# Two transformer layers in one kernel: the second batch stops preparing a third

## Chip, core and metric

The kernel runs on one core of one Trainium2 chip. The metric is the device time of one execution in microseconds (us), as the median of several runs. One more execution is taken with the hardware profiler; all rows below come from it.

## What is computed

Two layers on `x` of shape (2, 2048, 128), in float32. Each layer is an attention and a feed-forward part with adaptive layer norms (`mod` holds six rows for each batch) and residual adds. Cut to its steps:

```python
# layer 0
h = layernorm(x) * (1 + ca) + sa
Q, K, V = h @ Wq.T, h @ Wk.T, h @ Wv.T;  Q, K = rotate(Q), rotate(K)     # RoPE
x = x + ga * softmax(mask(Q @ K.T / sqrt(128), tril(k=1))) @ V
h = layernorm(x) * (1 + cb) + sb
x = x + gb * fp4_linear(silu(fp4_linear(h, w_gate)) * fp4_linear(h, w_up), w_down)
# layer 1
h = layernorm(x) * (1 + ca) + sa
x = x + ga * softmax(causal(h @ qk @ h.T / sqrt(128))) @ h @ ov
h = layernorm(x) * (1 + cb) + sb
x = x + gb * moe(h)      # 8 experts, top 2, each with one mean weight, plus a shared expert
```

## The kernel before

**Tiles and slots.** A batch has 2048 rows: 16 tiles of 128 rows, in 4 groups of 4. The queries of one tile are one slot. Slots 0 to 15 are the attention of layer 0, slots 16 to 31 that of layer 1, so a batch has 32 slots. The feed-forward part of layer 0 follows six and eight slots behind (`FFN_LAG`, `DOWN_LAG`), and norms and projections of later groups are spread over the slots by fixed slot numbers. All of it is written once for each engine in a loop `for b in range(BATCH)`, unrolled by Python, with BATCH = 2. After both batches the expert stage (moe) runs for all rows.

**In a slot.** PE computes the scores of the next slot in chunks of 512 keys (three passes for each chunk, `score_products`, L647), turns the probabilities of this slot (`turn_probs`, L755) and multiplies them with the values (`values`, L777). ACT computes the exponentials (`exp`, L1057) and copies what PE has turned out of the one PSUM bank TURN (`copy_probs`, L1083). DVE takes the maxima (`maximum`, L1357), adds the output to `x_sb` (`finish`, L1373) and does norms. POOL does the square roots for norms (`rsqrt`, L473).

**The order.** Each engine runs its own list in order. The scores of slot s+1 need the exponentials of slot s to have been read from the same banks (`exp_done`); transposes need bank TURN free again (`copied`). `TURN_AT` gives each turn of the bank its number in a batch (`turn_order`), and every wait on `turned` or `copied` counts `b * IN_TURN + TURN_AT[key]`. DVE's own order is counted by `dve_step`, 185 steps for each batch (`STEPS_PER_BATCH`).

**Preparing the next batch.** From slot 26 on, a batch starts layer 0 of the next one, `batch = BATCH - 1 - b`, so that the next batch finds its first group ready. NEXT_SLOT is 28. In order:

- slots 26 and 28: DVE `first_statistics` of groups 0 and 1 (L1220), POOL a square root for each
- slots 27 and 29: DVE `first_normalise` (L1227) of groups 0 and 1
- slot 28: PE turns the first group (key `"next"`, L595), ACT copies it to `hT` (L1029), PE `project_0(0, 0)` for the keys (L606), DVE `first_rotate` (L1237 to L1242)
- slot 29: PE `project_0(0, 1)` for the queries (L606), DVE `first_rotate`
- after slot 31: PE `first_values_and_scores` (L665, L647 to L659), then nine filler products `keep_clock(GATE, 9)` (L601), then the turning of layer 1's last norm group, key `("norm3", 3)`, and its router `logits` (L844). ACT copies the values (L998) and computes the first exponentials (`first_exp`, L1005); DVE takes the first maximum (L1291).

The second batch (b = 1) does all of this too, for batch 0 again; nothing reads the result.

After the last logits DVE adds the bias (L1437), ACT loads a table and computes the sigmoid (L1130), DVE picks the experts (L1507 to L1532), and meanwhile PE turns the expert weights (L888) and runs 17 fillers; then it turns the picks (L895), and the expert stage begins (L922).

Of the kernel before, what the change touches and what calls it, by code (L numbers as in the profile page):

```python
# [98 lines left out]

def input_turns(slot):  # L100

    firsts = (("fp4_in", FFN_LAG), ("norm2", DOWN_LAG + GROUP + 1), ("norm3", TILES + GROUP + 2))
    turns = [(kind, group_at(slot, first)) for kind, first in firsts if group_at(slot, first) is not None]
    if slot == NEXT_SLOT:
        turns.append(("next", 0))
    return turns if early_group(slot, K0_SLOT) is None else [("norm0", early_group(slot, K0_SLOT))] + turns
# [23 lines left out]

def turn_order():


    order = []
    for s in range(SLOTS):
        order += input_turns(s)
        for c in range(len(turn_chunks(*divmod(s, TILES)))):
            order.append(("probs", s, c))
            if c == 0 and ffn_tile(s, DOWN_LAG) is not None:
                order.append(("hq", s - DOWN_LAG))  # L140
    return order + [("norm3", GROUPS - 1)]


TURN_AT = {key: n + 1 for n, key in enumerate(turn_order())}
IN_TURN = len(TURN_AT)

# [9 lines left out]
parts_before, MAX_PARTS = before(lambda l, i: len(score_chunks(l, i)) if len(score_chunks(l, i)) > 1 else 0)  # L156
STEPS_PER_BATCH = 185


def build(nc, x, cos, sin, wq, wk, wv, w_gate, w_up, w_down, c0, wmod0, qk, ov, gate_w, lb_bias,  # L160
          e_gate, e_up, e_down, s_gate, s_up, s_down, c1, wmod1, out):
    ctx = ExitStack()
    with ctx:
# [276 lines left out]
        def _(pool):  # L440
# [43 lines left out]
            for b in range(BATCH):  # L484
# [12 lines left out]
                def hq_scaled(n):  # L497
                    pool.wait_ge(hq_grid, b * TILES + n + 1)
                    if n >= 2:
                        pool.wait_ge(turned, b * IN_TURN + TURN_AT["hq", n - 2] + 1)  # L500
                    pool.tensor_tensor(hq[:, n % 2, :], ha[:], hp[:], ALU.add).then_inc(hq_step, 1)  # L501
                    pool.wait_ge(hq_step, b * 2 * TILES + 2 * n + 1)
                    pool.tensor_tensor(hq[:, n % 2, :], hq[:, n % 2, :], hp[:], ALU.subtract).then_inc(hq_step, 1)
                    pool.wait_ge(hq_step, b * 2 * TILES + 2 * n + 2)
                    blocks = hq[:, n % 2, :].rearrange("p (k e) -> p k e", e=BLOCK)
                    pool.tensor_tensor(blocks, blocks, qh[:, 2, :].unsqueeze(2).to_broadcast(
                        [P, INNER // BLOCK, BLOCK]), ALU.mult).then_inc(hq_ready, 1)

                def xq_scaled(g):
                    pool.wait_ge(xq_grid, b * GROUPS + g + 1)  # L510
                    if g >= 1:
                        pool.wait_ge(turned, b * IN_TURN + TURN_AT["fp4_in", g - 1] + 1)
                    pool.tensor_tensor(xq[:], qa[:], qp[:], ALU.add).then_inc(xq_step, 1)
                    pool.wait_ge(xq_step, b * 2 * GROUPS + 2 * g + 1)
                    pool.tensor_tensor(xq[:], xq[:], qp[:], ALU.subtract).then_inc(xq_step, 1)
                    pool.wait_ge(xq_step, b * 2 * GROUPS + 2 * g + 2)
                    blocks = xq[:].rearrange("p (k e) -> p k e", e=BLOCK)
                    pool.tensor_tensor(blocks, blocks, qs[:, 2, :].unsqueeze(2).to_broadcast(
                        [P, GROUP * P // BLOCK, BLOCK]), ALU.mult).then_inc(xq_ready, 1)
# [13 lines left out]
                def keys_low(g):  # L533

                    cols = slice(g * BANK, (g + 1) * BANK)
                    pool.wait_ge(copied, b * IN_TURN + TURN_AT["norm2", g] + 1)
                    pool.tensor_tensor(h_parts[1][:, cols], hT[:, cols], h_parts[0][:, cols].bitcast(F32),
                                       ALU.subtract).then_inc(keys_ready, 1)

                for s in range(SLOTS):  # L540
# [13 lines left out]
                    if early_group(s, NORM0_SLOT) is not None:  # L554
                        rsqrt(2, early_group(s, NORM0_SLOT))
                    if s in (NEXT_SLOT - 2, NEXT_SLOT):
                        rsqrt(2, GROUPS + (s == NEXT_SLOT))
# [16 lines left out]
        def _(pe):  # L574
# [105 lines left out]
            for b in range(BATCH):  # L680
                def bank_free(key):

                    pe.wait_ge(copied, b * IN_TURN + TURN_AT[key])

                def out_of_bank(key):

                    pe.wait_ge(copied, b * IN_TURN + TURN_AT[key] + 1)

# [20 lines left out]
                def project_0_in(s):  # L709
# [13 lines left out]
                    if q is not None:  # L723
                        pe.wait_ge(roped, b * 4 * GROUPS + 4 * q + 2)
                        project_0(q, 1)
                    if s == NEXT_SLOT:
                        out_of_bank(("next", 0))
                        pe.wait_ge(logits_sum, b * GROUPS + GROUPS - 2)
                        project_0(0, 0)
                    if s == NEXT_SLOT + 1:  # L730
                        pe.wait_ge(roped, (b + 1) * 4 * GROUPS + 2)
                        project_0(0, 1)
# [102 lines left out]
                def logits(g):  # L835
                    out_of_bank(("norm3", g))
                    if g == 0:
                        pe.wait_ge(gu_used, b * TILES + TILES)
                    if g >= GROUPS - 2:
                        pe.wait_ge(roped, (b + 1) * 4 * GROUPS + 4)  # L840
# [8 lines left out]
                for s in range(SLOTS):  # L849
                    following = len(score_chunks(*divmod(s + 1, TILES))) if s + 1 < SLOTS else 0  # L850
                    n = len(turn_chunks(*divmod(s, TILES)))
                    for key in input_turns(s):
                        turn_group(key)
# [22 lines left out]
                pe.wait_ge(logits_sum, b * GROUPS + GROUPS - 1)  # L876
                first_values_and_scores(b, b * -1 + (BATCH - 1))
                keep_clock(GATE, 9)
                turn_group(("norm3", GROUPS - 1))
                pe.wait_ge(v_ready, (b + 1) * 2 * GROUPS + 1)  # L880
                logits(GROUPS - 1)


            pe.wait_ge(moe_w_loaded, 16 * 6)
            pe.wait_ge(logits_sum, BATCH * GROUPS)
            pe.wait_ge(copied, BATCH * IN_TURN + 1)
            for n in range(3 * UNITS):
# [70 lines left out]
        def _(act):  # L958
# [51 lines left out]
            for b in range(BATCH):  # L1010
                def filled(key):

                    act.wait_ge(turned, b * IN_TURN + TURN_AT[key] + 1)

# [34 lines left out]
                def exp(s, c):  # L1049
                    start, width = score_chunks(*divmod(s, TILES))[c]  # L1050
                    if c == 0:
                        act.wait_ge(max_ready, b * SLOTS + s + 1)
                        if s >= 2:
                            last = len(turn_chunks(*divmod(s - 2, TILES))) - 1
                            act.wait_ge(turned, b * IN_TURN + TURN_AT["probs", s - 2, last] + 1)
                    width = min(width, SEQ - start)
# [43 lines left out]
                for s in range(SLOTS):  # L1100
# [4 lines left out]
                    if n > 1:  # L1105
                        exp(s, 1)
                    for key in input_turns(s):
                        copy_group(key)
# [5 lines left out]
                    for c in range(max(n, turns)):  # L1114
# [6 lines left out]
                        if c + 2 < n:  # L1121
                            exp(s, c + 2)
                put_v_at(0, (b + 1) * 2 * GROUPS)
                copy_group(("norm3", GROUPS - 1))
                first_exp(b)
                act.wait_ge(copied, b * IN_TURN + IN_TURN + 1)

# [46 lines left out]
        def _(dve):  # L1174
# [3 lines left out]
            def link(ins):  # L1178

                steps[0] += 1  # L1180
                ins.then_inc(dve_step, 1)
                dve.wait_ge(dve_step, steps[0])
# [111 lines left out]
            first_maximum(-1)  # L1294
            setup_steps = steps[0]

            for b in range(BATCH):
                count = [0]

                def link(ins):  # L1300
                    count[0] += 1
                    ins.then_inc(dve_step, 1)
                    dve.wait_ge(dve_step, b * STEPS_PER_BATCH + setup_steps + count[0])

                def x_tile(t, n=1):
# [126 lines left out]
                def take_logits(g):  # L1432

                    dve.wait_ge(copied, b * IN_TURN + TURN_AT["norm3", g] + 1)
                    dve.tensor_copy(hT_all[:, bass.ds(b * SEQ + g * BANK, BANK)], hT_group[:])
# [16 lines left out]
                for s in range(SLOTS):  # L1452
# [9 lines left out]
                    if ffn_tile(s, FFN_LAG) is not None:  # L1462
                        combine(s - FFN_LAG)
                    if s in (NEXT_SLOT, NEXT_SLOT + 1):
                        first_rotate(b, s - NEXT_SLOT, link)
                    for c in range(1, following):
                        maximum(s + 1, c)
                    normalise_in_slot(s)
                    if s in (NEXT_SLOT - 1, NEXT_SLOT + 1):
                        first_normalise(b, BATCH - 1 - b, int(s > NEXT_SLOT))  # L1470
                    if ffn_tile(s, FFN_LAG) is not None:
                        quantise_h(s - FFN_LAG)
                    if early_group(s, NORM0_SLOT) is not None:
                        norm_0_statistics(early_group(s, NORM0_SLOT))
                    if s in (NEXT_SLOT - 2, NEXT_SLOT):
                        first_statistics(BATCH - 1 - b, int(s == NEXT_SLOT), link)
# [5 lines left out]
                normalise_in_slot(SLOTS + 1)  # L1482
                first_maximum(b)
                take_logits(GROUPS - 1)

                in_loop = count[0]
            assert in_loop == STEPS_PER_BATCH, in_loop

            steps[0] = setup_steps + BATCH * STEPS_PER_BATCH

            def link(ins):
                steps[0] += 1
                ins.then_inc(dve_step, 1)
                dve.wait_ge(dve_step, steps[0])


# [142 lines left out]
```

## Time and profile before

| | us |
|---|---|
| median of 3 runs | 732.59 |
| lowest, highest run | 732.2, 740.7 |
| profiled execution, whole | 740.21 |
| its span in the trace | 738.4 |

| engine | busy us | share of the span |
|---|---|---|
| PE | 647.3 | 88% |
| PE weight load | 504.9 | 68% |
| DVE | 511.4 | 69% |
| ACT | 319.5 | 43% |
| POOL | 222.5 | 30% |

The mean granted clock of PE is 0.948 of full speed. PE's products overlap one another, and their ends are modelled; the distance from one start to the next tells more than the length of one. The first batch runs to about 329 us, the second to about 620 us, the expert stage from about 634 us to the end.

### The profile page before, as it was taken

How to read it: one execution, taken by the hardware profiler on the slowest of the kernel's cores; microseconds unless marked ns; L12 is line 12 of the kernel's file. 1: busy time of each engine (PE TensorE's matmuls, PEld its weight loads, DVE VectorE, ACT ScalarE, POOL GpSimd, SP SyncE). 2: the span in 40 equal slices, each digit the busy share in tenths (PEclk: the TensorE clock that was granted, in tenths of full speed). 3: DMA queues.
4: the chain of work that ended last, by engine and by line, in shares of the span. 5: the costliest groups of instructions: out<-in, count | busy, mean ns of one | idle time of the engine just before them, and what ended most of it. 6: DMA issues, size and time to landing. Idle time of an engine off the chain costs nothing.

```text
span 738.4 us, 11039 instructions
## 1 busy us (share of the span) xinstructions
PE 647.3 (88%) x3816; PEld 504.9 (68%) x3828; DVE 511.4 (69%) x1465; ACT 319.5 (43%) x644; POOL 222.5 (30%) x225
## 2 busy tenths in 40 slices
PE   5889799988777999988889989958889998799997
PEld 4456687877556778775678777846677786576674
DVE  5957598696768667726669777596865754876665
ACT  1133344445234454543344444523445453554453
POOL 3333654343545211004455435253421102000000
PEclk9989999999879999999999999978999999999999
DMA  8400000000000000000000000000000000000001
GB/s 262 110 0 1 2 1 1 1 0 1 1 0 1 1 1 1 1 1 1 1 1 1 1 1 2 1 1 0 1 1 1 1 1 1 0 16 29 14 19 40
DMA packets 12078, 9.64 MB, mean 13 GB/s; under 512 B 1708, under 2 KB 10744, under 8 KB 12024
## 3 DMA queue, kind: packets, MB, share of 16 engines
q1 hardware_dynamic: 12024, 8.94, 4.1%
q8 instruction: 31, 0.51, 0.3%
q14 instruction: 23, 0.19, 0.1%
HBM read 6.84 MB, written 2.10 MB: 12 GB/s over the span
## 4 chain that ended last, share of the span: by engine, by line
PE 69%; DVE 18%; ACT 5%; POOL 4%; issue 4%; DMA 1%; SPq 0%; ACTq 0%; POOLq 0%
PE ps L777 14%; PE ps L647 12%; PE ps L755 8%; PE ps L606 5%; DVE xn L1320 5%; PE ps L922 4%; PE ps L924 4%; PE ps L923 4%; PE ps L800 3%; PE ps L665 2%; PE ps L801 2%; PE ps L595 2%; PE ps L816 2%; DVE row_max L1357 1%; PE ps L601 1%
## 5 line engine op out<-in xcount | busy, mean ns | idle before, releaser
L1083 ACT ACTIVATE probsT<-ps 128x512 f32<-128x512 f32 (+3 forms) x160 | 85.2, 533 | 180.4 <-PE ps L755 180.4
L777 PE MATMUL ps<-v_sb,probsT 128*128 128x129 f32 (+1 forms) x1148 | 157.1, 280 | 3.7 <-ACT probsT L1085 3.7
L777 PEld LDWEIGHTS ps<-v_sb,probsT 128*128 128x128 f32 (+1 forms) x1148 | 141.5, 191 | 10.6 <-ACT probsT L1085 5.5
L1357 DVE TENSOR_REDUCE row_max<-ps 128x1 f32<-128x512 f32 (+2 forms) x144 | 87.6, 619 | 48.3 <-PE ps L647 18.1
L755 PE MATMUL ps<-ident,probs 128*128 128x128 f32 (+1 forms) x574 | 95.7, 285 | 16.7 <-ACT probsT L1083 6.0
L755 PEld LDWEIGHTS ps<-ident,probs 128*128 128x128 f32 (+1 forms) x574 | 67.5, 143 | 49.0 <-issue 45.3
L1057 ACT ACTIVATE probs<-ps,neg_max 128x512 f32<-128x512 f32 (+7 forms) x158 | 92.8, 618 | 16.9 <-DVE neg_max L1364 16.0
L473 POOL TENSOR_TENSOR rstd<-veps,half 128x4 f32<-128x4 f32 x34 | 34.2, 1012 | 154.1 <-DVE veps L1211 153.9
L501 POOL TENSOR_TENSOR hq<-ha,hp 128x352 f32<-128x352 f32 x32 | 29.9, 934 | 139.5 <-DVE hp L1398 139.5
L647 PE MATMUL ps<-k_high,q_high 128*128 128x512 f32 (+4 forms) x112 | 46.0, 411 | 0.6 <-ACT probs L1005 0.6
L1152 ACT ACTIVATE probs<-ps 128x512 f32<-128x512 f32 x40 | 24.0, 599 | 44.7 <-PE ps L924 44.7
L1320 DVE TENSOR_SCALAR xn<-x_sb,mv,rstd 128x128 f32<-128x128 f32 x112 | 41.4, 435 | 2.2 <-POOL rstd L473 2.2
L1590 DVE TENSOR_TENSOR probs<-probs,ps 128x512 f32<-128x512 f32 x40 | 27.5, 687 | 19.9 <-ACT probs L1152 19.4
L1412 DVE SCALAR_TENSOR_TENSOR silu_g<-silu_g,ps 128x352 f32<-128x352 f32 x32 | 16.5, 516 | 34.1 <-ACT silu_g L1065 34.1
L922 PE MATMUL ps<-q_high,h_high 128*128 128x512 f32 x80 | 38.8, 485 | 0.8 <-DVE q_high L1523 0.8
L1372 DVE RECIPROCAL rsum<-ps 128x1 f32<-128x1 f32 x64 | 10.4, 163 | 40.8 <-PE ps L777 40.5
L647 PE MATMUL ps<-k_high,q_low 128*128 128x512 f32 (+4 forms) x112 | 38.7, 345 | 0.0
L647 PE MATMUL ps<-k_low,q_high 128*128 128x512 f32 (+4 forms) x112 | 38.3, 342 | 0.0
L647 PE MATMUL ps<-h_high,q_high 128*128 128x512 f32 (+2 forms) x80 | 36.9, 461 | 0.5 <-ACT probs L1057 0.5
L595 PE MATMUL ps<-ident,xn 128*128 128x128 f32 x100 | 17.6, 304 | 18.9 <-DVE xn L1320 18.0
L800 PE MATMUL ps<-w_guT,xqT 128*128 128x352 f32 x64 | 29.8, 553 | 4.6 <-ACT v_sb L998 2.5
L924 PE MATMUL ps<-q_high,h_low 128*128 128x512 f32 x80 | 32.2, 403 | 0.0
(240 smaller groups left out, 1380.8 us busy)
## 6 DMA issues: line engine op xcount, KB each, us to landing
out<-x_sb SPq DMA_DIRECT2D x8, 256.0 KB, 2.3
x_sb<-in_L_attn_x SPq DMA_DIRECT2D x2, 512.0 KB, 5.3
hT_all<-in_L_wmod SPq DMA_DIRECT2D x2, 384.0 KB
rope_cos<-table_cos SPq DMA_DIRECT2D x1, 768.0 KB, 7.5
rope_sin<-table_sin SPq DMA_DIRECT2D x1, 768.0 KB, 9.1
rope_cos<-table_cos SPq DMA_DIRECT2D x1, 256.0 KB, 4.1
rope_sin<-table_sin SPq DMA_DIRECT2D x1, 256.0 KB, 5.1
moe_raw<-in_L_ffn_expert_gate_w SPq DMA_DIRECT2D x1, 256.0 KB, 4.2
```

The costliest lines, as they stand in the source:

```text
L473: pool.tensor_tensor(rstd[:, kind, :], veps[:, kind, :], half[:], ALU.pow).then_inc(rstd_ready[kind], 1)
L606: pe.matmul(bank(dst), w[:], hT[:, g * BANK:(g + 1) * BANK], start=True, stop=True).then_inc(proj_ready, 1)
L647: mm = pe.matmul(ps[:, cols], q_parts[q][:, tile], keys[k][:, cols], start=(n == 0), stop=(stop and n == len(passes) - 1))
L755: mm = pe.transpose(bank(TURN, k * P, (k + 1) * P, size), probs[:, s % 2, j * P:j * P + size], ident[:])
L777: mm = pe.matmul(bank(OUT_AT, 0, V_W), probsT[0:size, n % 4, k * P:(k + 1) * P], v_sb[0:size, j, :], start=(c == 0 and k == 0), stop=(c == ...
L800: pe.matmul(bank(GATE, 0, INNER), lhs, w_guT[:, 0:INNER], start=True, stop=True)
L922: pe.matmul(dst, weights[0], high, start=start, stop=False)
L924: return pe.matmul(dst, weights[1], high, start=False, stop=stop)
L1057: act.activation(probs[:, s % 2, start:start + width], ps[:, start:start + width], ACT.Exp, bias=neg_max[:, s % 2:s % 2 + 1]).then_inc(exp ...
L1083: ins = act.activation(probsT[:, n % 4, 0:full], bank(TURN, 0, full), ACT.Copy)
L1320: ins = dve.tensor_scalar(xn[:, g, t * P:(t + 1) * P], x_tile(g * GROUP + t), mv[:, kind, t, 0:1], rstd[:, kind, t:t + 1], ALU.subtract, A ...
L1357: ins = dve.tensor_reduce(dst, ps[:, start:start + width], AX.X, ALU.max, negate=single)
```

## The change

All preparation of a next batch gets the condition `b + 1 < BATCH`: in the second batch there are no such statistics, square roots, normalisations, turn, copy, projections, rotations, values, scores, maximum or exponentials, and no waits on them. The nine filler products stay. Since the two batches now differ in their number of turns and of DVE steps, the turns are numbered over both batches, and DVE's steps are counted through. Cut to its core:

```diff
-def input_turns(slot):
+def input_turns(batch, slot):
...
-    if slot == NEXT_SLOT:
+    if slot == NEXT_SLOT and batch + 1 < BATCH:
         turns.append(("next", 0))
...
-TURN_AT = {key: n + 1 for n, key in enumerate(turn_order())}
-IN_TURN = len(TURN_AT)
+TURN_AT = {key: n + 1 for n, key in enumerate([(b, *key) for b in range(BATCH) for key in turn_order(b)])}
+ALL_TURNS = len(TURN_AT)
...
# POOL
-                    if s in (NEXT_SLOT - 2, NEXT_SLOT):
+                    if b + 1 < BATCH and s in (NEXT_SLOT - 2, NEXT_SLOT):
                         rsqrt(2, GROUPS + (s == NEXT_SLOT))
...
# PE
-                    if s == NEXT_SLOT:
+                    if b + 1 < BATCH and s == NEXT_SLOT:
                         out_of_bank(("next", 0))
                         pe.wait_ge(logits_sum, b * GROUPS + GROUPS - 2)
                         project_0(0, 0)
-                    if s == NEXT_SLOT + 1:
+                    if b + 1 < BATCH and s == NEXT_SLOT + 1:
                         pe.wait_ge(roped, (b + 1) * 4 * GROUPS + 2)
                         project_0(0, 1)
...
-                    if g >= GROUPS - 2:
+                    if b + 1 < BATCH and g >= GROUPS - 2:
                         pe.wait_ge(roped, (b + 1) * 4 * GROUPS + 4)
...
                 pe.wait_ge(logits_sum, b * GROUPS + GROUPS - 1)
-                first_values_and_scores(b, b * -1 + (BATCH - 1))
+                if b + 1 < BATCH:
+                    first_values_and_scores(b, b + 1)
                 keep_clock(GATE, 9)
                 turn_group(("norm3", GROUPS - 1))
-                pe.wait_ge(v_ready, (b + 1) * 2 * GROUPS + 1)
+                if b + 1 < BATCH:
+                    pe.wait_ge(v_ready, (b + 1) * 2 * GROUPS + 1)
                 logits(GROUPS - 1)
...
# ACT
-                put_v_at(0, (b + 1) * 2 * GROUPS)
+                if b + 1 < BATCH:
+                    put_v_at(0, (b + 1) * 2 * GROUPS)
                 copy_group(("norm3", GROUPS - 1))
-                first_exp(b)
-                act.wait_ge(copied, b * IN_TURN + IN_TURN + 1)
+                if b + 1 < BATCH:
+                    first_exp(b)
+                act.wait_ge(copied, TURN_AT[b, "norm3", GROUPS - 1] + 1)
...
# DVE
-                    if s in (NEXT_SLOT, NEXT_SLOT + 1):
+                    if b + 1 < BATCH and s in (NEXT_SLOT, NEXT_SLOT + 1):
                         first_rotate(b, s - NEXT_SLOT, link)
...
-                    if s in (NEXT_SLOT - 1, NEXT_SLOT + 1):
+                    if b + 1 < BATCH and s in (NEXT_SLOT - 1, NEXT_SLOT + 1):
                         first_normalise(b, BATCH - 1 - b, int(s > NEXT_SLOT))
...
-                    if s in (NEXT_SLOT - 2, NEXT_SLOT):
+                    if b + 1 < BATCH and s in (NEXT_SLOT - 2, NEXT_SLOT):
                         first_statistics(BATCH - 1 - b, int(s == NEXT_SLOT), link)
...
-                first_maximum(b)
+                if b + 1 < BATCH:
+                    first_maximum(b)
```

## Rows read from the trace of the kernel before

**Rows 1.** The page, part 1: busy us (share of the span) xinstructions of each engine.

```profile
PE 647.3 (88%) x3816; PEld 504.9 (68%) x3828; DVE 511.4 (69%) x1465; ACT 319.5 (43%) x644; POOL 222.5 (30%) x225
```

**Rows 2.** Busy time by stretch: us, each engine's busy us (xcount), PE's granted clock, DMA share.

```profile
577.00:606.00 29.00, 28.32 (x186) 22.70 (x185) 20.66 (x61) 14.39 (x26) 2.01 (x2) 1.00 0.00 1
606.00:616.00 10.00, 9.15 (x75) 8.07 (x76) 3.07 (x18) 4.15 (x7) 1.01 (x1) 1.00 0.00 1
616.00:620.00 4.00, 2.35 (x17) 1.61 (x15) 1.65 (x7) 1.25 (x3) 0.46 (x1) 1.00 0.00 0
```

**Rows 3.** Chain that ended last, slots 28 and 29: start us, us, what.

```profile
576.86 0.45 PE ps L595 x4
577.34 0.79 ACT hT L1029
578.17 1.98 PE ps L606 x4
580.15 0.44 PE ps L755 x4
...
586.75 0.79 PE ps L647 x3
587.53 1.72 PE ps L606 x4
589.25 0.44 PE ps L755 x4
```

**Rows 4.** Timeline, PE and ACT in slots 28 and 29: start us, us [idle before].

```profile
575.57 1.27 ACT L1057 ACTIVATE probs<-ps,neg_max 128x512 f32<-128x512 f32 x2 [0.28 <-DVE neg_max L1364]
...
578.17 1.12 PE L606 MATMUL ps<-hT,wkT 128*128 128x512 f32 x2 [0.17 <-ACT hT L1029]
...
585.84 1.26 ACT L1057 ACTIVATE probs<-ps,neg_max 128x512 f32<-128x512 f32 x2
...
586.57 0.50 PE L647 MATMUL ps<-h_high,q_high 128*128 128x512 f32 x1
```

**Rows 5.** Timeline, DVE in slot 28.

```profile
579.33 0.69 DVE L1237 TENSOR_TENSOR rope_t<-ps,rope_cos 128x512 f32<-128x512 f32 x1 [0.21 <-PE ps L606]
...
584.61 0.42 DVE L1357 TENSOR_REDUCE row_max<-ps 128x1 f32<-128x256 f32 x1 [0.61 <-PE ps L653]
```

**Rows 6.** Chain that ended last, end of the second batch.

```profile
613.17 0.36 DVE x_sb L1373
...
614.67 1.02 POOL rstd L473
615.71 1.12 DVE xn L1320 x4
...
618.45 1.04 PE ps L844 x8
```

**Rows 7.** Timeline, PE at the end of the second batch.

```profile
612.77 1.06 PE L665 MATMUL ps<-wv_g,hT 128*128 128x128 f32 x8
...
614.59 1.89 PE L601 MATMUL ps<-unpick,ident_b 128*128 128x512 bf16 x8
...
616.88 0.66 PE L595 MATMUL ps<-ident,xn 128*128 128x128 f32 x4 [0.41 <-DVE xn L1320]
...
619.81 2.72 PE L888 MATMUL ps<-ident,moe_raw 128*128 128x128 f32 x15 [0.33 <-issue]
```

**Rows 8.** Busy time by stretch of 1 us, columns as in rows 2.

```profile
620.00:621.00 1.00, 1.00 (x9) 1.00 (x8) 0.00 (x0) 1.00 (x1) 1.00 (x1) 0.78 0.08 16
621.00:622.00 1.00, 1.00 (x7) 1.00 (x6) 0.43 (x2) 0.49 (x2) 1.00 (x1) 0.50 0.00 0
```

**Rows 9.** PE at a granted clock of 0.50, slot 16: table by stretch, then timeline.

```profile
488.00:491.00 3.00, 1.11 (x4) 0.71 (x4) 0.50 0.00 0
488.50 1.11 PE L595 MATMUL ps<-ident,xn 128*128 128x128 f32 x4 [3.60 <-DVE xn L1320]
```

**Rows 10.** Timeline, PE's weight loads behind the fillers.

```profile
627.37 1.79 PEld L895 LDWEIGHTS ps<-ident_b,xn 128*128 128x128 bf16 x32 [0.88 <-DVE xn L1532]
```

More of the change, by code:

```diff
@@ L128, in ffn_tile, with turn_order @@
     return slot - lag if 0 <= slot - lag < TILES else None
-def turn_order():
+def turn_order(batch):
     order = []
     for s in range(SLOTS):
-        order += input_turns(s)
+        order += input_turns(batch, s)
         for c in range(len(turn_chunks(*divmod(s, TILES)))):
@@ L156 @@
 parts_before, MAX_PARTS = before(lambda l, i: len(score_chunks(l, i)) if len(score_chunks(l, i)) > 1 else 0)
-STEPS_PER_BATCH = 185
 def build(nc, x, cos, sin, wq, wk, wv, w_gate, w_up, w_down, c0, wmod0, qk, ov, gate_w, lb_bias,
@@ L499, in hq_scaled @@
                     if n >= 2:
-                        pool.wait_ge(turned, b * IN_TURN + TURN_AT["hq", n - 2] + 1)
+                        pool.wait_ge(turned, TURN_AT[b, "hq", n - 2] + 1)
                     pool.tensor_tensor(hq[:, n % 2, :], ha[:], hp[:], ALU.add).then_inc(hq_step, 1)
@@ L511, in xq_scaled @@
                     if g >= 1:
-                        pool.wait_ge(turned, b * IN_TURN + TURN_AT["fp4_in", g - 1] + 1)
+                        pool.wait_ge(turned, TURN_AT[b, "fp4_in", g - 1] + 1)
                     pool.tensor_tensor(xq[:], qa[:], qp[:], ALU.add).then_inc(xq_step, 1)
@@ L535, in keys_low @@
                     cols = slice(g * BANK, (g + 1) * BANK)
-                    pool.wait_ge(copied, b * IN_TURN + TURN_AT["norm2", g] + 1)
+                    pool.wait_ge(copied, TURN_AT[b, "norm2", g] + 1)
                     pool.tensor_tensor(h_parts[1][:, cols], hT[:, cols], h_parts[0][:, cols].bitcast(F32),
@@ L681, in bank_free @@
                 def bank_free(key):
-                    pe.wait_ge(copied, b * IN_TURN + TURN_AT[key])
+                    pe.wait_ge(copied, TURN_AT[b, *key])
                 def out_of_bank(key):
-                    pe.wait_ge(copied, b * IN_TURN + TURN_AT[key] + 1)
+                    pe.wait_ge(copied, TURN_AT[b, *key] + 1)
                 def turn_group(key):
@@ L851, in _ @@
                     n = len(turn_chunks(*divmod(s, TILES)))
-                    for key in input_turns(s):
+                    for key in input_turns(b, s):
                         turn_group(key)
@@ L885, in _ @@
             pe.wait_ge(logits_sum, BATCH * GROUPS)
-            pe.wait_ge(copied, BATCH * IN_TURN + 1)
+            pe.wait_ge(copied, ALL_TURNS + 1)
             for n in range(3 * UNITS):
@@ L1011, in filled @@
                 def filled(key):
-                    act.wait_ge(turned, b * IN_TURN + TURN_AT[key] + 1)
+                    act.wait_ge(turned, TURN_AT[b, *key] + 1)
                 def copy_group(key):
@@ L1054, in exp @@
                             last = len(turn_chunks(*divmod(s - 2, TILES))) - 1
-                            act.wait_ge(turned, b * IN_TURN + TURN_AT["probs", s - 2, last] + 1)
+                            act.wait_ge(turned, TURN_AT[b, "probs", s - 2, last] + 1)
                     width = min(width, SEQ - start)
@@ L1106, in _ @@
                         exp(s, 1)
-                    for key in input_turns(s):
+                    for key in input_turns(b, s):
                         copy_group(key)
@@ L1294, in _ @@
             first_maximum(-1)
-            setup_steps = steps[0]
             for b in range(BATCH):
[L1298 to L1303, printed above, removed]
                 def x_tile(t, n=1):
@@ L1432, in take_logits @@
                 def take_logits(g):
-                    dve.wait_ge(copied, b * IN_TURN + TURN_AT["norm3", g] + 1)
+                    dve.wait_ge(copied, TURN_AT[b, "norm3", g] + 1)
                     dve.tensor_copy(hT_all[:, bass.ds(b * SEQ + g * BANK, BANK)], hT_group[:])
@@ L1482, in _ @@
                 normalise_in_slot(SLOTS + 1)
-                first_maximum(b)
+                if b + 1 < BATCH:
+                    first_maximum(b)
                 take_logits(GROUPS - 1)
[L1486 to L1494, printed above, removed]
             def over_experts(t):
```

## Prediction, made before the change was run

> **What bounds the kernel now.** I began with the busy shares of the page: TensorE (PE) is busy for 647.3 of 738.4 us and no other engine comes near it [rows 1]. That is an average over stages, so it doesn't say what the few instructions of this change are worth. The second view is the table of busy time by stretch, laid over the end of the second batch [rows 2]. Slots 28 and 29 and the turn into slot 30 lie in 577 to 606 us: PE is busy 28.32 of 29.00 us, VectorE (DVE) 20.66, ScalarE (ACT) 14.39. PE has no room there, so an instruction taken from PE should come off the time at full price, and one taken from DVE or ACT should not. From 616 to 620 us it is the reverse: PE is busy 2.35 of 4.00 us, and the stretch is a chain of short steps over four engines. From 634 us to the end the expert stage runs; nothing of the change lies in it.
>
> The third view is the chain of work that ended last, in order of time. It shows the work for the batch that doesn't exist on the path, twice [rows 3]. In slot 28: four transposes (0.45 us), ACT's copy to `hT` (0.79), the four pieces of `project_0(0, 0)` (1.98), then the slot's ordinary transposes at 580.15. In slot 29: three score passes (0.79), the four pieces of `project_0(0, 1)` (1.72), the ordinary transposes at 589.25. The fourth view is the timeline, to see who else would stop PE once these are gone [rows 4, 5].
>
> **The change part by part.** The sum is made against the profiled span of 738.4 us; the profiled execution took 740.21 us and the runs have a median of 732.59 us. The edit takes microseconds and no share of a loop, so I carry the same number of microseconds over to the median.
>
> *Slot 28, PE.* From the start of the removed transposes at 576.86 to the start of the ordinary ones at 580.15 are 3.29 us [rows 3]. What stays of it are the score passes of tile (29, 0). They are the same shape as those at 586.75, 0.79 us. The rest, 3.29 - 0.79 = 2.50 us, is removed: 0.45 for turning, 1.98 for projecting, and 0.07 of waiting for ACT's copy, which by the timeline was up to 0.17 at that place [rows 4]. Gain 2.50 us.
>
> *Slot 29, PE.* `project_0(0, 1)` stands between score passes and transposes, all back to back: 589.25 - 587.53 = 1.72 us [rows 3]. Gain 1.72 us. Together 4.22 us.
>
> *Who would stop PE instead.* With the projection gone PE comes earlier to the transposes of slot 28, which need the exponentials (28, 0). ACT did (28, 0) and (28, 1) as one pair of 1.27 us that began at 575.57, so it ends at 576.84 [rows 4]. PE asks for them after the score passes, at about 576.86 + 0.79 = 577.65. Cover 0.8 us. In slot 29 the pair begins at 585.84 and lasts 1.26, ending at 587.10. PE needs the first of it for its score passes at 586.57, half-way through the pair (586.47), with 0.1 us to spare, and needs the second after the transposes at about 587.5 + 0.4, with 0.8 us to spare. Everything in these two places moves earlier by the same 2.50 us, so the margins stay. The thin one is 0.1 us: if ACT gained less than PE, PE would wait there, up to the 2.50 us of slot 28. ACT itself loses the 0.78 us copy and gains no work, so I take the full gain.
>
> *DVE.* It loses two sets of statistics, two normalisations and two rotations. Such a rotation starts at 579.33 us and the reductions wait behind it, but the last reduction of the same slot at 584.61 us still finds DVE idle for 0.61 us, waiting for PE's mask product [rows 5]. So DVE had caught up before its result was wanted, and this work was hidden under PE. Worth nothing here; its cover would be gone only if PE got more than 0.61 us ahead inside one slot. PE does get 2.50 us ahead in slot 28, but DVE loses the rotation, far more than that, in the same slot. GpSimd (POOL) loses two square roots in slots in which it mostly idles: nothing.
>
> *The end of the batch.* PE loses `first_values_and_scores`: values from 612.77 us, scores until the nine `keep_clock` products begin, their group starting at 614.59 [rows 7]. These are about 614.59 - 612.77 = 1.8 us of PE. They run beside the chain that decides: DVE takes the last tile at 613.17, POOL's square root 614.67 (1.02 us), DVE normalises 615.71 (1.12), PE turns 616.88 (0.66) [rows 7], ACT copies in the 0.91 us between, PE's logits 618.45 (1.04) [rows 6]. PE ended its filler at 614.59 + 1.89 = 616.48 and then waited 0.41 us for DVE [rows 6, 7]. Taking work away before a wait only lengthens the wait. Also DVE's maximum, ACT's copy to `v_sb` and first exponential lie in idle time beside this chain: nothing. Gain zero.
>
> *What that wait may cost.* The nine filler products now start and end 1.8 us earlier relative to the chain. So PE's thin stretch before the next dense work, the turning of the expert weights at 619.81, grows from 619.8 - 616.5 = 3.3 us to 5.1 us [rows 7]. In the kernel before, the granted clock was 1.00 (2.4 GHz) up to 620 us, 0.78 in the microsecond after it, a mix of the two levels, and 0.50 (1.2 GHz) in the next, after this thin stretch [rows 2, 8]. If the fall comes 1.8 us earlier with the filler's end, it comes near 618.3 us and catches the eight logits products, which are on the chain. Their price at the lower level isn't in the trace. The nearest row is one of four transposes at a granted clock of 0.50: 1.11 us, against 0.66 at 616.88, so 0.11 us more for each [rows 7, 9]. Eight logits products: up to 8 x 0.11 = 0.9 us; with the four transposes also caught, 0.9 + 0.45 = 1.35 us. Lower bound 0, since the fall may as well come where it did. I take 0.6 us, most of the logits at the lower clock, because the end of the filler is what moves.
>
> The Trainium skill, "TensorE: Matmul & The Clock Gate", section "What's actually happening", says that the throttled state is the default and activity releases it. By that rule taking useless products away has a price of its own; the trace agrees so far as the fall at 620 us follows PE's thinnest stretch. By the opposite reading, that only useful waits matter, the tail would be free and the sum 0.6 us better.
>
> Behind the logits a low clock is covered. PE turns the expert weights and runs 17 fillers until about 627 us, and its next product then still waited 0.88 us for DVE [rows 10]. DVE's routing chain decides there and has no PE in it. The start of the expert stage follows an idle of PE in either kernel and should be what it is.
>
> Sum: -2.50 - 1.72 + 0.6 = -3.6 us. 732.6 - 3.6 = **729.0 us**, 0.5% less. A measurement of this kernel can tell about 2% from no change, so this will read as the same.
>
> **Rivals.**
> 1. *Forecast:* PE's time in slots 28 and 29 comes off whole, the logits pay part of it back: 729.0 us. Chance 0.58.
> 2. *The tail is free:* the clock falls where it did. 732.6 - 4.2 = 728.4 us. For it: the fall need not follow the filler. Chance 0.15.
> 3. *Colder everywhere in the tail:* turning and logits at 1.2 GHz (+1.35), and the expert stage's first products stay there longer as well. That place has no row here, so I take as much again as in the tail: 732.6 - 4.2 + 2 x 1.35 = 731.1 us. This is the skill's rule (same page and section as above) carried to its end. Against it: PE's idle before the expert stage isn't touched. Chance 0.14.
> 4. *Hidden anyway:* PE only waits longer for exponentials, since ACT and DVE set the pace of the slots. 732.6 us. For it: the 0.1 us margin in slot 29. Against it: PE busy 28.32 of 29.00 us [rows 2], and DVE idle before its last reduction [rows 5]. Chance 0.06. That the change does nothing at all is ruled out: the removed rows are in the trace of the second batch.
> 5. *Slower:* the clock falls during the dense end of slot 31 and of the tail. Dense work at 1.2 GHz costs its own length again, so it decides from 4.2 us of dense work on the path; 8 us of it would give 732.6 - 4.2 + 8 = 736.4 us. Its place would be 606 to 616 us. Against it: PE is busy 9.15 of 10.00 us there at a granted clock of 1.00 [rows 2], and nothing is taken out between 589 and 612 us. Chance 0.04.
> 6. The three runs shown spread from 732.2 to 740.7 us; that the median of the new kernel falls on a high one gives 740.7 - 3.6 = 737 us. Chance 0.03.
>
> **Numbers.** Cases 1 to 4 lie between 728.4 and 732.6 us. Below, 1 us for more gain (a shorter cold start of the expert stage, the 0.17 us wait) and the runs' own 0.4 us; above, the same 1 us. That makes 727 to 733.5 us, with the forecast's own range 728 to 730.5. Faster by over 2% would need 14.7 us, more than all removed PE work: 0.01. Slower by over 2%: half the upper tail of case 6 at most, 0.01. Within 2%: 0.98.
>
> **What would show it.** In the new trace no projection product in the second batch's slots 28 and 29; in slot 28 the ordinary transposes 0.8 us after the score passes begin instead of behind a projection; the distance from the last reduction of slot 27 to PE's last values product of slot 31 shorter by 4.2 us; PE's wait for DVE before the turning of group 3 up from 0.41 to about 2.2 us; the granted clock already below 1.00 in the microsecond of the logits, and their group longer than 1.04 us. Wrong would be: a wait of PE for ACT's exponentials in slot 29, a distance shortened by less than 3.5 us, or a clock below 1.00 before the end of slot 31.

## The result, and the profile after

| | before | changed |
|---|---|---|
| median of 20 runs, us | 737.78 | 732.62 |
| lowest, highest | 732.2, 741.46 | 728.88, 738.18 |
| profiled execution, span | 738.4 | 732.8 |

The ratio changed to before is 0.9944, with a 95% interval from 0.9918 to 0.9969. The kernel became faster by 0.56%, between 0.3 and 0.8%. In microseconds of the new median of before that is 737.78 x 0.0056 = 4.1 us, between 2.3 and 6.0. The three runs from which the prediction started, with their median of 732.59, were a low draw from a broad spread; over twenty runs the median of the same kernel is 5 us higher. Four runs of the later comparisons took 921 to 2102 us, against 728 to 743 us for all others, and stand in no figure below.

The page's first part of the changed kernel, to be held against [rows 1]: PE has 9.4 us less to do, and DVE 11.2.

```profile
span 732.8 us, 10947 instructions
...
PE 637.9 (87%) x3800; PEld 499.3 (68%) x3800; DVE 500.2 (68%) x1426; ACT 317.9 (43%) x641; POOL 220.5 (30%) x223
```

The two spans differ by 5.6 us. To see where, I cut both traces at places that exist in each. The first two are the starts of the groups of 16 values products in slots 27 and 31 in the chain that ended last. Before:

```profile
575.02 1.84 PE ps L777 x16
...
611.08 1.86 PE ps L777 x16
```

and in the changed kernel:

```profile
572.90 1.84 PE ps L776 x16
...
604.66 1.86 PE ps L776 x16
```

The distance between them, A, went from 36.06 to 31.76 us. B goes from there to DVE's bias add behind the last logits, C from the bias add to the first product of the expert stage, D from that to the end of the span. All in us:

| trace | start of slot 27's 16 | A | B | C | D |
|---|---|---|---|---|---|
| before | 575.02 | 36.06 | 8.44 | 14.22 | 104.66 |
| changed | 572.90 | 31.76 | 9.23 | 14.22 | 104.69 |

So of 5.6 us, 2.1 arise before the start of the 16 products of slot 27; 4.3 are gained in A; 0.8 are lost in B; C and D are alike. The 2.1 us are no gain of the change. Up to there PE's work is the same in both kernels, and of the removed work only slot 26's statistics on DVE and one square root on POOL lie ahead. From DVE's output add of slot 22 to that of slot 27 both kernels take 35.79 us, and all fourteen traces of this document 35.78 or 35.79.

A is the forecast gain. These are the places of [rows 3] in the chain of the changed kernel. No projection is left. In slot 28 the ordinary transposes come 0.69 us behind the 16 products, where 3.29 us lay between; in slot 29 they come 0.78 us after the score passes begin, where it was 0.79 + 1.72 us.

```profile
574.75 0.69 PE ps L646 x3
575.44 0.44 PE ps L754 x4
...
582.03 0.78 PE ps L646 x3
582.81 0.44 PE ps L754 x4
```

B is the forecast price. The chain at the end of the second batch in the changed kernel, against [rows 6]: up to the turning of group 3 every step is as long as before to 0.01 us; the logits then take 1.89 us in place of 1.04.

```profile
606.75 0.36 DVE x_sb L1368
...
608.24 1.02 POOL rstd L472
...
609.28 1.13 DVE xn L1315 x4
...
610.46 0.67 PE ps L594 x4
...
611.15 0.79 ACT hT_group L1034
...
611.98 1.89 PE ps L843 x8
```

PE's timeline and the table by stretch show what goes with it, against [rows 7, 8]. PE waits 2.01 us for DVE, where it waited 0.41, and the granted clock has fallen to 0.50 (1.2 GHz) when the logits begin:

```profile
610.46 0.66 PE L594 MATMUL ps<-ident,xn 128*128 128x128 f32 x4 [2.01 <-DVE xn L1315]
611.98 1.87 PE L843 MATMUL ps<-router_T,hT_group 128*128 128x8 f32 x8 [0.87 <-ACT hT_group L1034]
...
610.00:611.00 1.00, 0.55 (x4) 0.42 (x4) 0.40 (x2) 0.00 (x0) 0.00 (x0) 1.00 0.00 0
611.00:612.00 1.00, 0.13 (x3) 0.02 (x1) 0.04 (x1) 0.78 (x1) 0.00 (x0) 0.95 0.00 0
612.00:613.00 1.00, 1.00 (x5) 1.00 (x6) 0.38 (x1) 0.00 (x0) 0.00 (x0) 0.50 0.00 0
```

### The profile page after: what moved, and what is told of

Its sections match the earlier page's. It is cut to its first block, busy times and chain, and to the rows that moved or that the text cites. A ratio compares the mean times of both kernels' runs of the same rounds, so it can differ in the third digit from the quotient of the medians.

```text
span 732.8 us, 10947 instructions
## 1 busy us (share of the span) xinstructions
PE 637.9 (87%) x3800; PEld 499.3 (68%) x3800; DVE 500.2 (68%) x1426; ACT 317.9 (43%) x641; POOL 220.5 (30%) x223
## 4 chain that ended last, share of the span: by engine, by line
PE 65%; DVE 21%; ACT 5%; POOL 4%; issue 4%; DMA 1%; SPq 0%; ACTq 0%; POOLq 0%
PE ps L776 14%; PE ps L646 12%; PE ps L754 8%; DVE xn L1315 5%; PE ps L923 4%; PE ps L925 4%; PE ps L924 4%; PE ps L605 4%; PE ps L799 3%; PE ps L800 2%; PE ps L664 2%; PE ps L815 2%; PE ps L594 2%; DVE row_max L1352 1%; DVE xn L1230 1%
## 5 line engine op out<-in xcount | busy, mean ns | idle before, releaser
L472 POOL TENSOR_TENSOR rstd<-veps,half 128x4 f32<-128x4 f32 x32 | 32.2, 1013 | 152.3 <-DVE veps L1214 152.1
L815 PE MATMUL ps<-w_dg,hqT 128*128 128x128 f32 (+1 forms) x192 | 28.2, 283 | 4.5 <-ACT hqT L1071 4.5
```

The costliest lines, as they stand in the source:

```text
L472: pool.tensor_tensor(rstd[:, kind, :], veps[:, kind, :], half[:], ALU.pow).then_inc(rstd_ready[kind], 1)
L815: mm = pe.matmul(bank(OUT_AT, DOWN.start, DOWN.stop), hqT[0:size, k * P:(k + 1) * P], w_dg[0:size, bass.ds(b, 1), k, :].rearrange("p a n - ...
```

## The experiments

The spread of the runs, some 9 us, is larger than any step asked about, so each experiment was read by its distances A to D, in one trace each; the times stand beside them. Each ratio is against runs of the kernel before on the same chip.

**The changed kernel three more times.** No edit.

> The changed kernel once more, beside the others. Three distances in the trace are compared in all runs, since they don't depend on what happened earlier: A, from the start of the 16 values products of slot 27 to the start of the 16 values products of slot 31 (before 36.06 us, changed 31.76); B, from there to DVE's bias add behind the last logits (before 8.44, changed 9.23); C, from the bias add to the first product of the expert stage (14.22 in both). Theory 1 (PE's removed work is the gain, the clock at the logits is the price): A 31.8, B 9.2 if the granted clock falls before the logits, 8.4 if it doesn't. Rival (both differences are scatter of one execution): A and B anywhere between the two kernels' values.

> The changed kernel as a partner of these three on the same chip. A 31.8 us; B 9.2 or 8.4 as the logits are at 0.50 or 1.00. The time of an execution should go with its mean granted clock as in the 20 runs known (728.9 us at 0.961 to 738.2 at 0.948), and in the traces the difference between executions should lie ahead of slot 27, in stretches with a granted clock under 1.00, and in A, C and D by under 0.3 us.

> The changed kernel on this chip: A 31.8 us, B 8.4 or 9.2, C 14.2, D 104.6 to 105.4. The start of slot 27's 16 values products follows the time at the lower clock ahead of it, 0.2 to 0.3 us for each us of it (570.5 us at 44.2 us of it, 574.7 at 61.2).

| trace | start of slot 27's 16 | A | B | C | D | ratio, interval |
|---|---|---|---|---|---|---|
| second | 571.04 | 31.78 | 9.25 | 14.22 | 104.71 | 0.9942, 0.9911 to 0.9974 |
| third | 574.75 | 31.78 | 8.43 | 14.22 | 104.62 | 0.9928, 0.9902 to 0.9954 |
| fourth | 571.96 | 31.75 | 9.24 | 14.23 | 104.72 | 0.9948, 0.9917 to 0.9978 |

A is the same to 0.03 us in four traces. B has two values, and the logits' own line says which: in the third trace, with the same wait of 2.01 us ahead, the clock had not yet fallen, and they took 1.06 us.

```profile
612.33 0.66 PE L594 MATMUL ps<-ident,xn 128*128 128x128 f32 x4 [2.01 <-DVE xn L1315]
613.86 1.06 PE L843 MATMUL ps<-router_T,hT_group 128*128 128x8 f32 x8 [0.87 <-ACT hT_group L1034]
```

**The kernel before twice more.** No edit.

> The kernel before again, for its trace. All runs so far, put at the same time at the lower clock, give 5.2 us between the two kernels, and the distances A and B explain 3.5 to 4.3. If one of the distances of the kernel before varies between executions, this trace and the next show it: A 36.06, B 8.4 or 9.2 to 9.3 as the logits are at 1.00 or 0.50, C 14.22, D 104.5 to 105.4. If all are as in the first trace, what is missing lies ahead of slot 27 or in the scatter.

> The kernel before once more; A, B, C, D as in the run before it, with B at 9.2 in at least one of the four traces that have the old end of the batch if the clock's fall before the logits isn't particular to the changed kernel.

The second trace has its 16 products of slot 27 at 570.93 us, A 36.10, B 8.44, C 14.22, D 104.71; the third has 576.05, 36.10, 8.44, 14.22, 104.69. Every distance repeats; what varies is the arrival at slot 27, by 5.1 us. The same kernel against itself gave ratios of 0.9981 (0.9953 to 1.0009) and 0.9980 (0.9943 to 1.0018), so 0.2% can come of nothing. The table by stretch, over the first 570 us of the third and of the second trace, shows with what the arrival goes, the granted clock, 0.94 and 0.96:

```profile
0.00:570.00 570.00, 492.43 (x3007) 387.07 (x3009) 401.76 (x1225) 238.43 (x507) 215.47 (x221) 0.94 0.04 13
```

```profile
0.00:570.00 570.00, 493.01 (x3039) 388.15 (x3042) 405.04 (x1234) 240.47 (x510) 216.27 (x221) 0.96 0.04 13
```

The later trace has done less work by 570 us. Taken up to each trace's own slot 27, DVE is busy for 404.95 and 405.04 us and ACT for 240.76 and 240.79, but PE for 498.40 and 493.94. By the clock's own records, the fourteen traces spent 44 to 68 us of that stretch at the lower level, and the arrival is later by 0.22 us for each such us (correlation 0.95). The expectation for the changed kernel's fourth trace, 0.2 to 0.3 us for each, was met by the set and not by the trace itself: with 54.6 us at the lower level it arrived at 571.96 us, where the rule and its two anchors give 572.6 or later.

**Only the slots' part removed.** The work at the end of the batch stays, on old contents of its tiles; the output doesn't use it.

```diff
-                if b + 1 < BATCH:
-                    first_values_and_scores(b, b + 1)
+                first_values_and_scores(b, BATCH - 1 - b)
...
-                if b + 1 < BATCH:
-                    first_exp(b)
+                first_exp(b)
```

> Only the preparation in slots 26 to 29 is gone; values, scores, maximum and exponentials of the batch that doesn't exist stay at the end (on old contents of their tiles), and so the filler products end where they did. Theory 1: A 31.8 us as in the changed kernel, B 8.4 us as before, logits at a granted clock of 1.00, so 0.8 us less than the changed kernel and 4.2 less than before. Rival (removing the end's work is what saves, or B's growth has another cause): B 9.2 with the logits products 0.1 us longer each.

A 31.78, B 8.49, C 14.23, D 105.35 us; ratio 0.9934 (0.9898 to 0.9969). PE waited 0.41 us for DVE as in the kernel before, and the logits ran at full clock:

```profile
610.15 1.03 PE L845 MATMUL ps<-router_T,hT_group 128*128 128x8 f32 x8 [0.96 <-ACT hT_group L1034]
```

A and B are as theory 1 has them. D was 0.7 us longer, which I hadn't expected, and took back what B had saved: A to D sum to 159.85 us, against 159.90 in the changed kernel. D comes back below.

**Only the end's part removed.** The conditions on NEXT_SLOT are taken out again.

```diff
-                    if b + 1 < BATCH and s == NEXT_SLOT:
+                    if s == NEXT_SLOT:
                         out_of_bank(("next", 0))
```

> Only the values, scores, maximum and exponentials at the end are gone, 1.8 us of PE; the preparation in slots 26 to 29 stays. Theory 1: A 36.1 us as before, B 9.2 us, so this removal alone makes the kernel 0.8 us slower. Rival (work of PE taken away can't cost): B 8.4 or less.

A 36.10, B 9.34, C 14.23, D 104.53 us; ratio 1.0004 (0.9969 to 1.0040). The trace says 0.9 us slower in B, where 0.8 was expected; the turning was slower too, 0.76 us for 0.66. The interval of the runs, 0.7% wide, can't tell 0.1%, so the slowdown is shown in the trace and not in the times.

```profile
612.80 0.76 PE L594 MATMUL ps<-ident,xn 128*128 128x128 f32 x4 [2.01 <-DVE xn L1315]
614.43 1.87 PE L843 MATMUL ps<-router_T,hT_group 128*128 128x8 f32 x8 [0.87 <-ACT hT_group L1034]
```

**DVE's share put back into the changed kernel.** POOL's square roots and the normalisations come back in the same way as the statistics.

```diff
-                    if b + 1 < BATCH and s in (NEXT_SLOT - 2, NEXT_SLOT):
+                    if s in (NEXT_SLOT - 2, NEXT_SLOT):
                         first_statistics(BATCH - 1 - b, int(s == NEXT_SLOT), link)
...
+                    if b + 1 == BATCH and s in (NEXT_SLOT, NEXT_SLOT + 1):
+                        idle_rotate(s - NEXT_SLOT)      # five operations of 128x512
```

> The changed kernel with DVE's and POOL's share of the preparation put back: statistics, square roots and normalisations in slots 26 to 29, and for each rotation five operations of 128x512 on DVE that read the tables in place of PE's result. PE and ACT do nothing more. Theory 1 (DVE's share was hidden): A 31.8 us, at most 0.2 more. Rival (DVE's share was part of the gain and PE's 4.2 us are overstated, since PE waited for DVE's maxima): A 33 to 35 us.

A 33.10 us, B 9.24, C 14.24, D 104.67; ratio 0.9955 (0.9922 to 0.9987). Theory 1 fell here; 33.10 is just inside the rival's range. The chain that ended last runs on DVE alone from 574.03 to 590.24 us, where in the changed kernel it runs on PE. The timeline of slots 28 and 29 shows DVE late: its last maximum of slot 28 is done at 581.2, ACT's exponentials begin 0.78 us late, and PE stands in front of the score passes for 0.71 us.

```profile
576.77 0.69 DVE L1237 TENSOR_TENSOR rope_t<-rope_cos,rope_sin 128x512 f32<-128x512 f32 x1
...
579.41 1.62 DVE L1364 TENSOR_REDUCE row_max<-ps 128x1 f32<-128x512 f32 x3
...
581.25 1.27 ACT L1058 ACTIVATE probs<-ps,neg_max 128x512 f32<-128x512 f32 x2 [0.78 <-DVE neg_max L1371]
581.99 0.50 PE L646 MATMUL ps<-h_high,q_high 128*128 128x512 f32 x1 [0.71 <-ACT probs L1058]
```

**Its mirror: only DVE's and POOL's share removed from the kernel before.** PE turns and projects old contents of the first group, ACT copies.

```diff
-                    if kind in ("norm0", "next"):
+                    if kind == "norm0" or kind == "next" and b + 1 < BATCH:
                         pe.wait_ge(xn0_ready, ...)
...
+                    if s == NEXT_SLOT + 1:      # PE: projects, but waits for no rotation when b is 1
                         project_0(0, 1)
```

> The kernel before, with only DVE's and POOL's share of the preparation in slots 26 to 29 gone (statistics, square roots, normalisations, rotations); PE still turns old contents of the first group and projects twice, ACT still copies, and the end of the batch is as before. The mirror of the run that put DVE's share back into the changed kernel, where distance A (slot 27's to slot 31's 16 values products) was 33.10 us in place of 31.78. Theory (DVE's share was covered as long as PE had its own extra 4.3 us, and becomes the bound only when those are gone): A 36.0 to 36.1 us, no gain alone. Rival (DVE's share is worth its 1.3 us in either kernel): A 34.8 us.

A 36.11, B 8.48, C 14.22, D 104.66 us; ratio 0.9984 (0.9951 to 1.0016). DVE's share alone, with POOL's, is worth nothing. So DVE's share and PE's don't add: 0 for DVE alone, 36.10 - 33.10 = 3.0 us for PE and ACT alone, 4.3 us for both. DVE was the second limit, 3.0 us behind PE. One reserve: the rotations put back don't wait for PE's projections, as the real ones did, so 3.0 us is measured for this stand-in.

**More filler.** Three kernels, each built on the one before it: 18 filler products in place of 9; six more between the turning and the logits; and fillers in PE's idle stretch ahead of the expert stage.

```diff
-                keep_clock(GATE, 9)
+                keep_clock(GATE, 9 if b + 1 < BATCH else 18)
                 turn_group(("norm3", GROUPS - 1))
+                if b + 1 == BATCH:          # second kernel
+                    keep_clock(GATE, 6)
...
+            keep_clock_small(12)            # third kernel
+            pe.wait_ge(unselT_ready, 1)
+            keep_clock(0, 10)
             pe.wait_ge(totals_ready, 1)
...
+            keep_clock(0, 3)
```

> The changed kernel with 18 filler products in place of 9 at the end of the second batch: 9 x 0.215 = 1.9 us more, so that they end where they did before relative to the chain. Distance B (from the 16 values products of slot 31 to DVE's bias add) was 8.44 us before and 9.23 in the changed kernel. Theory 1 (the thin stretch of PE before the logits brings the clock's fall forward): logits at 1.00 again, B 8.4 to 8.5. Rival (the fall comes with where the execution happens to stand, and not with PE's load): B 9.2 as often as not.

> As with 18 fillers, and six more between the turning of group 3 and its logits, while ACT copies. Theory 1: B 8.4 to 8.5; and the clock stays at 1.00 behind the logits too, where it fell in the kernel before, which changes no time, as DVE's routing decides there: C 14.2 us. If the six overrun the copy, B grows by at most 0.2.

> As the one before, and fillers in PE's idle stretch ahead of the expert stage: 12 narrow ones, 10 of 512 columns once the first half of the masks is copied, 3 behind the sums. In both kernels the first products of the expert stage run at 0.50 for about 3.3 us. Theory: with PE kept at work the stage starts at 1.00; the distance D from its first product to the end of the span (104.66 us before, 104.69 changed) falls by up to 1.6 us, C stays 14.2 or grows by up to 0.3. Rival (DVE's second weight split and its mean weights decide the start of the stage): D falls by under 0.5 us.

| kernel | A | B | C | D | ratio, interval |
|---|---|---|---|---|---|
| 18 fillers | 31.78 | 8.43 | 14.22 | 104.62 | 0.9923, 0.9892 to 0.9954 |
| and six in the gap | 31.78 | 8.59 | 14.22 | 105.41 | 0.9946, 0.9915 to 0.9977 |
| and before the experts | 31.78 | 8.59 | 14.23 | 104.60 | 0.9937, 0.9911 to 0.9964 |

With 18 fillers PE had no wait at all ahead of the turning and B is 8.43, but one of the four traces of the changed kernel has that value too, so this one trace alone proves little. What counts is the set. In the five traces with the old end of the batch (before three times, only the slots' part removed, only DVE's share removed) the logits ran at 1.00, B 8.44 to 8.49. In the six with 9 fillers and nothing ahead of them (changed four times, only the end's part removed, DVE's share put back) five ran at 0.50, B 9.23 to 9.34. In the three with more filler none did. The set speaks against the rival too, by which the fall comes wherever the execution happens to stand: then some of the eight others should have been at 0.50. The six fillers in the gap overran ACT's copy and cost 0.16 us. They didn't keep the clock up behind the logits, as expected of them: over 618.09 to 622.09 us it was 0.69, and 0.50 from there into the expert stage. C was 14.22 all the same.

The third kernel did keep the clock up. This is its table by stretch over the start of the expert stage, at 1.00 throughout, where the changed kernel's has 0.62 for the first 4 us:

```profile
626.00:630.00 4.00, 3.90 (x19) 2.38 (x17) 3.69 (x12) 1.86 (x3) 0.00 (x0) 1.00 0.00 0
630.00:634.00 4.00, 2.62 (x12) 1.66 (x11) 3.31 (x6) 1.23 (x2) 0.00 (x0) 1.00 0.00 0
```

```profile
628.00:632.00 4.00, 3.89 (x11) 2.78 (x12) 3.69 (x12) 0.69 (x2) 0.00 (x0) 0.62 0.00 0
```

And yet D is 104.60. The faster PE only stands sooner, at 632.11 us, where DVE is late with its first product of the stage, behind its second weight split and its mean weights:

```profile
631.37 1.28 DVE L1587 TENSOR_TENSOR probs<-probs,ps 128x512 f32<-128x512 f32 x2
...
632.11 0.51 PE L935 MATMUL ps<-q_high,h_high 128*128 128x512 f32 x1 [1.38 <-DVE probs L1587]
```

The rival held. Against the kernel that it was built on, with D at 105.41, the third did give 0.81 us; against the changed kernel's 104.62 to 104.72 it gave 0.02 to 0.12. D does grow when the low clock covers the first 4 us of the stage whole, as in the kernel with six fillers in the gap (D 105.41; only the slots' part removed 105.35): then PE is the later one. In the other twelve traces D lies between 104.53 and 104.72.

```profile
625.00:629.00 4.00, 3.91 (x9) 2.81 (x9) 3.69 (x12) 0.69 (x2) 0.00 (x0) 0.50 0.00 0
```

By the traces 18 fillers give up to 0.8 us over the changed kernel. The times can't show it: medians of 733.68 us against 735.07 for the changed kernel on the same chip, with intervals that overlap nearly whole.

## Why the prediction was right and where it was wrong

**The step that failed: "a measurement of this kernel can tell about 2% from no change, so this will read as the same".** No row of the prediction stands behind the 2%. Twenty runs of each kernel gave an interval of 0.25% to either side, and the ratio, 0.9944 (0.9918 to 0.9969), is clear of 1: a gain that the prediction's own rows established, -3.6 us or 0.5%, was called "the same", and the runs showed it as a gain of 0.56%, 4.1 us. The chance of 0.98 for "within 2%" says nothing false about the size.

**Right: PE's work on the path.** The sum had 2.50 + 1.72 = 4.22 us. A shrank by 4.30, and by 4.28 to 4.35 in every pair of traces. Slot 28 gave 3.29 - 0.69 = 2.60 us, since its score passes take 0.69 and not the 0.79 borrowed from slot 29; slot 29 gave 2.50 - 0.78 = 1.72. Reading each gain from what stood between two neighbouring groups of the chain, and leaving the score passes in, was the right method. PE's margins for exponentials held: no wait for ACT in slots 28 and 29 of the changed kernel.

**Right: the end's work hides, and its loss has a price.** PE waited 2.01 us (said 2.2). Of the nine fillers [rows 7] shows eight, so their true start in the kernel before lies some 0.2 us ahead of 614.59, and the removed work was 1.6 us and not 1.8. The clock fell at 611.9 us, ahead of the logits, which is 618.3 on the old scale (said near 618.3), and they took 0.83 us more (said 0.6, up to 0.9). B grew by 0.79 us, so A and B together gave 3.51 us in this pair, against the forecast 3.6. By the Trainium skill, "TensorE: Matmul & The Clock Gate", section "What's actually happening", the throttled state is the default and activity releases it. Three of four traces agree, with logits of 1.87 to 1.88 us behind the longer wait; the fourth, with 1.06 us behind the same wait, shows no fall there, and its tail was free. Not foreseen was that the same kernel does either. Rival 3 went too far: the turning of group 3 kept its 0.66 us, and D did not grow.

**Half right: DVE's share "worth nothing here".** The prediction read 0.61 us of idle DVE before the last maximum, named the condition under which that cover would go, and said that the condition isn't met because DVE loses its rotation in the same slot. That holds for the change as made, so the total was right for its reason and not by luck. But the label was wrong: DVE's removal was needed for 1.3 us of the 4.3. Had the change taken only PE's part, 3.0 us would have come. By the prediction's own rows one would estimate 2.50 - 0.61 = 1.9 us lost in slot 28 alone, so such a row gives the sign and not the size.

**Wrong: the level.** The time of 729.0 us was 3.6 us taken off 732.59, the median of three runs. Two things in sight spoke against that base: one of the three runs was 740.7, and the profiled execution took 740.21. Case 6 thought of the spread, but only for the new median, and gave it 0.03. Over all comparisons 140 runs of the kernel before average 738.1 us and 56 of the changed kernel 733.5. The measured 732.62 lay inside the range only since the range reached up to 733.5: that hit is luck.

**Open.** These means differ by 4.6 us, with a standard error of 0.4. The distances explain 4.3 less B's 0 to 0.8, so 3.5 to 4.3. The rest, 0.3 to 1.1 us, no distance shows. It may be scatter or a difference in how often the clock falls before slot 27; the traces are too few to say. Why the clock falls in one execution and not in another at the same place is open too.

## What to carry to other kernels

Dead work is worth what PE, or whoever sets the pace, spends on it between two steps of the chain, and the second limit close behind has to lose its share too: ask what idle time the next engine has before the result that is wanted, against what the first engine gains. That says who will be last; here it overstated by how much. Work that is removed ahead of a wait gave nothing here and took 0.8 us in most traces, where the clock fell in the longer wait. With a spread of 9 us between executions, compare distances between the same two instructions in several traces, and don't take a median of three as the level.

## What the runs showed of the hardware

The time of one kernel spreads by some 9 us, from 728.88 to 738.18 us in the twenty runs of the changed one, and goes with the mean granted clock of the execution. The five fastest, 728.9 to 729.3 us, had 0.961 to 0.966; the five slowest, 736.6 to 738.2 us, had 0.948 to 0.950. The traces cover part of that spread, and in them nearly all of it lies before slot 27, whose 16 values products began between 570.43 and 576.05 us in fourteen traces with the same work of PE ahead of them, 0.22 us later for each us spent at the lower clock. Whether the clock falls in a given short wait of PE differs between executions: in six traces the same 2.01 us ahead of the turning left the logits at 1.00 once and at 0.50 five times, 1.06 against 1.87 us for the eight products. And a stage may run its first products at 1.2 GHz for nothing, where another engine is the later one.
